# Keeping the gate's normalised rows and logits in SBUF for the experts' stage

## The reference

```python
logits = jnp.einsum('bsd,ed->bse', x, gate_w) + gate_b
probs = jax.nn.softmax(logits, axis=-2)            # over the 2048 tokens
vals, idx = top_k(probs, 8)                        # 8 tokens for each batch row and expert
tok = take_along_axis(x, idx)                      # rows of x
merged = jnp.einsum('bked,bke->bed', tok, vals)    # one row for each batch row and expert
h = gelu([merged, 1] @ w1[e])                      # w1: 32 x 257 x 1024
o = [h, 1] @ w2[e]                                 # w2: 32 x 1025 x 256
out = zeros.at[idx].add(o * vals)                  # back to the 8 tokens
```

## Time and profile before

| | |
|---|---|
| median of three runs | 5150.57 us |
| profiled execution: its span | 5142.3 us |
| median of the runs less this span (what lies around it) | 8.3 us |
| PE / DVE / ACT / POOL busy, share of the span | 92% / 82% / 67% / 26% |
| bytes moved by DMA | 498.42 MB |
| gate's stage | 575 to 755 us |
| experts' stage | 755 to 974 us |

### The profile page before, as it was taken

The page is one execution under the profiler, slowest core; times in us unless marked ns, Lnnn a source line. Parts: engine busy times, 40 slices in busy tenths (PEclk is TensorE's granted clock), DMA queues, the critical chain, the costliest instruction groups (busy, mean ns, idle before and its releaser), DMA issues. The chain is left out here.

```text
span 5142.3 us, 90411 instructions
## 1 busy us (share of the span) xinstructions
PE 4714.6 (92%) x34043; PEld 2092.5 (41%) x34043; DVE 4237.0 (82%) x5517; ACT 3449.7 (67%) x6176; POOL 1333.4 (26%) x881
## 2 busy tenths in 40 slices
PE   6999786797999999999999999999998879999993
PEld 3444452364333333333333333333334445555542
DVE  6999650397899999999999999999993877777736
ACT  4787310132688888888888888888886326666663
POOL 2233220164000000000000000000001229999992
PEclk9999897898899999999999999999998669999996
DMA  5110479688333333343333344333322941222305
GB/s 182 52 53 33 155 247 385 251 280 232 45 53 48 48 48 48 54 54 51 48 48 48 50 54 53 50 48 48 49 34 76 313 128 42 71 70 67 78 10 167
DMA packets 390773, 498.42 MB, mean 97 GB/s; under 512 B 165440, under 2 KB 278880, under 8 KB 373312
## 3 DMA queue, kind: packets, MB, share of 16 engines
q1 hardware_dynamic: 372448, 465.90, 38.7%
q10 hardware_dynamic: 17888, 26.74, 1.5%
HBM read 325.15 MB, written 165.02 MB: 95 GB/s over the span
## 5 line engine op out<-in xcount | busy, mean ns | idle before, releaser
L792 DVE TENSOR_REDUCE at_NM<-at_MX 128x1 f32<-128x1024 f32 (+1 forms) x3008 | 3085.0, 1050 | 299.5 <-PE at_MX L614 270.9
L734 ACT ACTIVATE at_PB<-at_S 128x512 f32<-128x512 f32 x5056 | 2719.4, 597 | 585.9 <-PE at_S L643 466.0
L614 PE MATMUL at_MX<-at_KT,at_QT 48*128 48x512 f32 (+1 forms) x5056 | 1919.7, 455 | 60.2 <-DMA at_VS<-v 45.6
L643 PE MATMUL at_S<-at_QT,at_KT 50*128 50x512 f32 (+1 forms) x5056 | 1899.9, 441 | 6.0 <-ACT at_PB L734 5.8
L655 PE MATMUL at_AV<-at_PB,at_VS 128*32 128x256 f32 (+1 forms) x18304 | 1567.7, 414 | 16.7 <-ACT at_AVS L742 15.7
L643 PEld LDWEIGHTS at_S<-at_QT,at_KT 50*128 50x128 f32 (+1 forms) x5056 | 801.8, 187 | 876.6 <-ACT at_PB L734 772.0
L614 PEld LDWEIGHTS at_MX<-at_KT,at_QT 48*128 48x128 f32 (+1 forms) x5056 | 791.6, 190 | 311.0 <-DVE at_NM L792 217.7
L655 PEld LDWEIGHTS at_AV<-at_PB,at_VS 128*32 128x32 f32 x18304 | 364.6, 108 | 858.6 <-ACT at_PB L734 745.4
L548 POOL CAST at_NMR<-at_NMF 16x128 fp32r<-16x128 f32 x79 | 22.1, 280 | 1625.3 <-ACT at_NMF L747 1625.3
L575 POOL TENSOR_TENSOR at_SUM<-at_SUM,at_PB 128x2048 f32<-128x2048 f32 x90 | 415.4, 4615 | 10.9
L932 PE MATMUL wkv_PQ<-wkv_XT,wkv_WT 128*128 128x512 f32 x768 | 339.6, 600 | 42.5 <-DVE wkv_DL L1052 25.9
(11 more groups left out here) (209 smaller groups left out, 3531.4 us busy)
## 6 DMA issues: line engine op xcount, KB each, us to landing
moe_W<-in_w SPq DMA_DIRECT2D x64, 1024.0 KB, 11.9
at_QT<-qk SPq DMA_DIRECT2D x402, 128.0 KB, 5.2
at_KT<-qk SPq DMA_DIRECT2D x384, 128.0 KB, 6.6
qk<-r_HI SPq DMA_DIRECT2D x52, 512.0 KB, 5.0
qk<-r_LO SPq DMA_DIRECT2D x52, 512.0 KB, 5.3
at_VS<-v SPq DMA_DIRECT2D x96, 256.0 KB, 9.2
at_KT<-qk SPq DMA_DIRECT2D x96, 256.0 KB, 6.2
ycat<-wkv_Y SPq DMA_DIRECT2D x32, 512.0 KB, 2.6
```

The costliest lines, as they stand in the source:

```text
L614: ins = nc.tensor.matmul(MX[r][:, a, :], q_of(s)[h:h + NQ, b * P:(b + 1) * P], k_of(it, s, b * P // W)[h:h + NQ, (c + a) * W:(c + a + 1) * W],
L643: nc.tensor.matmul(SP_[item(it, s, "score", t)[1]][:, :], k_of(it, s, c)[h:h + NQ + 2, kb * P:(kb + 1) * P], q_of(s)[h:h + NQ + 2, c * W:( ...
L734: nc.scalar.activation(PB[:, t % NPB, :], SP_[r][:, :], ACT.Exp, scale=scale).then_inc(exp_done, 1)
L792: nc.vector.tensor_reduce(NM4[:, b, c:c + 1], MX[r][:, :, :].rearrange("p a n -> p (a n)"), AX_X, ALU.max, negate=True).then_inc(ring_got, 1)
```

## The change

`rows`, a [128, 16, 4, 256] tile (64 KB in each partition), and `lg`, [128, 2048], are allocated around both stages. The gate's stage writes into them; the experts' stage reads them there. The DRAM tensors `xn2` and `logits`, their stores and their loads are gone. The bias GB now stands on all 128 partitions (four small loads), and PG has 128 rows, of which batch row b uses 32. After the merge the rows' space holds the second W2 buffer, HS, HT and OS, so `load(g)` is split, W2(1) waits for `merged`, and the clearing of HT waits for it too. The store of `routed` stands ahead of W2(1).

```diff
 # phase_gate
-        XN = [m.sb(f"XN{u}", [P, J, D]) for u in range(2)]
-        LG = [m.sb(f"LG{u}", [EXPERTS, GT]) for u in range(2)]
-        GB = m.sb("GB", [EXPERTS, 1])
-        PG = m.ps("PG", [EXPERTS, GT])
+        GB = m.sb("GB", [B * EXPERTS, 1])
+        PG = m.ps("PG", [B * EXPERTS, GT])
...
-            for dst, ap in ((ident[:, :], ident_d), (GW[:, :, :], ...), (GB[:, :], gb_d)):
+            for dst, ap in ((ident[:, :], ident_d), (GW[:, :, :], ...)):
                 sp.dma_start(dst, ap).then_inc(const_ld, 16)
+            for b in range(B):
+                sp.dma_start(GB[b * EXPERTS:(b + 1) * EXPERTS, :], gb_d).then_inc(const_ld, 16)
...
                 store(g)
-                if g > 0:
-                    store_normed(g - 1)
-                if g > 1:
-                    store_logits(g - 2)
-            store_normed(NGR - 1)
-            store_logits(NGR - 2)
-            store_logits(NGR - 1)
             for u in range(NX):
                 sp.wait_ge(x_st[u], 16 * len(range(u, NGR, NX)))
-            for u in range(2):
-                sp.wait_ge(n_st[u], 8 * NGR)
-                sp.wait_ge(l_st[u], 8 * NGR)
...
-                    ins = nc.tensor.matmul(PG[:, :], GW[:, c, :], XT[g % 2][:, c, :],
+                    ins = nc.tensor.matmul(PG[experts_of(g), :], GW[:, c, :], XT[g % 2][:, c, :],
...
+                es = experts_of(g)      # slice(g // E4 * EXPERTS, (g // E4 + 1) * EXPERTS)
                 wait(act, gated, g + 1)
-                wait(act, l_st[g % 2], 16 * (g // 2))
-                nc.scalar.activation(LG[g % 2][:, :], PG[:, :], ACT.Identity, bias=GB[:, 0:1]).then_inc(logits, 1)
+                nc.scalar.activation(lg[es, g % E4 * GT:(g % E4 + 1) * GT], PG[es, :], ACT.Identity,
+                                     bias=GB[es, 0:1]).then_inc(logits, 1)
...
                 wait(dve, rs1, g + 1)
-                wait(dve, turned, g - 1)
-                wait(dve, n_st[g % 2], 16 * (g // 2))
-                    ins = nc.vector.tensor_scalar(XN[g % 2][:, j, :], X[g % NX][:, j, :], ...
+                    ins = nc.vector.tensor_scalar(rows[:, g, j, :], X[g % NX][:, j, :], ...
 # phase_experts
-        XB = [m.sb(f"XB{u}", [P, B, 2, D]) for u in range(NX)]
-        W2 = [m.sb(f"W2{u}", [P, 4, HC, D]) for u in range(2)]
+        W2 = [m.sb("W20", [P, 4, HC, D]),
+              held_rows[:, 0:W2_END].rearrange("p (k c n) -> p k c n", k=4, c=HC)]
+        HS = held_rows[:, W2_END:HS_END]        # HT, OS behind it
...
-            def load(g):
-                u = g % 2
+            def load_w1(g):
                 wait(sp, h_put, g - 1)
...
+            def load_w2(g):
+                if g == 1:
+                    sp.wait_ge(merged, 1)
                 wait(sp, o_put, g - 1)
...
-            sp.dma_start(LG[:, :], lg_d.rearrange("b e t -> (b e) t")).then_inc(lg_ld, 16)
...
-            for g in range(2):
-                load(g)
+            load_w1(0)
+            load_w2(0)
+            load_w1(1)
             sp.wait_ge(w_done, 1)
             sp.dma_start(w_d.rearrange("b e t -> (b e) t"), LG[:, :]).then_inc(w_st, 16)
+            load_w2(1)
             for g in range(2, EG):
-                load(g)
+                load_w1(g)
+                load_w2(g)
...
+            pool.wait_ge(merged, 1)
             nc.gpsimd.memset(HT[:, :, :, :], 0.0).then_inc(zeroed, 1)
...
-            dve.wait_ge(lg_ld, 16)
             nc.vector.tensor_reduce(nmax[:, :], LG[:, :], AX_X, ALU.max, negate=True).then_inc(nmax_done, 1)
...
-            dve.wait_ge(zeroed, 6)
+            dve.wait_ge(zeroed, 5)      # the sixth ahead of the first copy to HT
...
-            for i in range(NX): load_x(i)            # and the other pairs after the exponential
...
-            for i in range(PAIRS):
-                wait(pe, x_ld[i % NX], 16 * B * (i // NX + 1))
-                ... XB[i % NX][:, b, k, :] ...
-                ins.then_inc(xb_used, 1)
+            for t in range(NB):
+                for b in range(B):
+                    ins = nc.tensor.matmul(PM[b * NE:(b + 1) * NE, 0:D], WTS[:, t, b * NE:(b + 1) * NE],
+                                           rows[:, b * E4 + t // J, t % J, :], start=(t == 0), stop=(t == NB - 1))
+            ins.then_inc(merged, 1)
```

More of the change, by code:

```diff
@@ L1114, with phase_gate @@
 HEADS2, DH2 = 8, 32
-def phase_gate(nc, y_d, ow_d, x_d, xnew_d, xn_d, ident_d, gw_d, gb_d, lg_d):
+def phase_gate(nc, y_d, ow_d, x_d, xnew_d, rows, lg, ident_d, gw_d, gb_d):
     E4 = T // GT
@@ L1147, in phase_gate, with experts_of @@
         x_ld, x_st = ([m.sem(f"{n}{u}") for u in range(NX)] for n in ("x_ld", "x_st"))
-        a_ld, n_st, l_st = ([m.sem(f"{n}{u}") for u in range(2)] for n in ("a_ld", "n_st", "l_st"))
+        a_ld = [m.sem(f"a_ld{u}") for u in range(2)]
         block = ctx.enter_context(nc.Block())
+        def experts_of(g):
+            return slice(g // E4 * EXPERTS, (g // E4 + 1) * EXPERTS)
         @block.sync
@@ L1166, in store @@
                 sp.dma_start(group(held(xnew_d), g), X[g % NX][:, :, :]).then_inc(x_st[g % NX], 16)
[L1168 to L1175, removed]
             sp.dma_start(OW[:, :, :], ow_d.rearrange("(q p) n -> p q n", p=P)).then_inc(ow_ld, 16)
@@ L1243, in turn @@
                         ins = nc.tensor.transpose(PT[:, c, j * P:(j + 1) * P],
-                                                  XN[g % 2][:, j, c * P:(c + 1) * P], ident[:, :])
+                                                  rows[:, g, j, c * P:(c + 1) * P], ident[:, :])
                     if c < CC - 1:
@@ L1259, in _ @@
             source(1)
[L1260 removed]
+            pe.wait_ge(const_ld, 16 * (2 + B))
             for g in range(NGR):
@@ L1325, in normed @@
                 wait(dve, rs1, g + 1)
[L1326 to L1327 removed]
                 for j in range(J):
[L1329 removed]
+                    ins = nc.vector.tensor_scalar(rows[:, g, j, :], X[g % NX][:, j, :], MV1[:, j, 0:1],
                                                   RS1[:, j:j + 1], ALU.subtract, ALU.mult)
@@ L2012, in _, with phase_experts @@
                 rope(g, 3)
-def phase_experts(nc, lg_d, xn_d, w1_d, w2_d, pick_d, ident_d, w_d, o_d):
+def phase_experts(nc, rows, LG, w1_d, w2_d, pick_d, ident_d, w_d, o_d):
     HID = 1024
@@ L2048, in phase_experts @@
         PO = m.ps("PO", [P, 512])
[L2049 to L2052, removed]
+        const_ld, nmax_done, zeroed, exp_done, soft, w_done, w_st, wt_put, wt_got = (m.sem(n) for n in (
+            "const_ld", "nmax_done", "zeroed", "exp_done", "soft", "w_done", "w_st", "wt_put", "wt_got"))
+        merged, ms_done, ms_turned, mts_done, me_done, pk_done, h_put, h_got, t_put, t_got, o_put, o_got, o_st = (
+            m.sem(n) for n in ("merged", "ms_done", "ms_turned", "mts_done", "me_done", "pk_done", "h_put", "h_got",
                                "t_put", "t_got", "o_put", "o_got", "o_st"))
         w1_ld, w2_ld = ([m.sem(f"{n}{u}") for u in range(2)] for n in ("w1_ld", "w2_ld"))
-        x_ld = [m.sem(f"x_ld{u}") for u in range(NX)]
-        xb_v = xn_d.rearrange("(b q p h i) d -> q h p b i d", b=B, p=P, h=J // 2, i=2)
         w1_v = w1_d[:, 0:D, :].rearrange("(g k) (c p) n -> g p k c n", k=4, p=P)
@@ L2113, in _ @@
                 nc.vector.tensor_copy(WTS[:, n * HC:(n + 1) * HC, :], TP[:, :, :]).then_inc(wt_got, 1)
-            dve.wait_ge(xb_used, PAIRS)
+            dve.wait_ge(merged, 1)
             nc.vector.tensor_copy(MS[:, :], PM[:, 0:D]).then_inc(ms_done, 1)
@@ L2149, in _ @@
         def _(act):
[L2150 to L2156, removed]
             act.wait_ge(nmax_done, 1)
@@ L2401, in sandwich @@
     ycat = dram("ycat", [2 * CC, P, TOK])
-    x1, xn2, x2, x3 = (dram(n, [TOK, D]) for n in ("x1", "xn2", "x2", "x3"))
-    logits, routed = (dram(n, [B, EXPERTS, T]) for n in ("logits", "routed"))
+    x1, x2, x3 = (dram(n, [TOK, D]) for n in ("x1", "x2", "x3"))
+    routed = dram("routed", [B, EXPERTS, T])
     expert_out = dram("expert_out", [B, EXPERTS, D])
@@ L2415, in sandwich @@
         phase_wkv(nc, xnT, d["rkv_w"], d["decay"], d["first"], ident, ycat)
-        phase_gate(nc, ycat, d["out_w"], d["x"], x1, xn2, ident, d["gate_w"], d["gate_b"], logits)
-        phase_experts(nc, logits, xn2, d["w1"], d["w2"], d["pick"], ident, routed, expert_out)
+        with nc.sbuf_tensor("rows", [P, NG, J, D], F32) as rows, nc.sbuf_tensor("lg", [B * EXPERTS, T], F32) as lg:
+            phase_gate(nc, ycat, d["out_w"], d["x"], x1, rows, lg, ident, d["gate_w"], d["gate_b"])
+            phase_experts(nc, rows, lg, d["w1"], d["w2"], d["pick"], ident, routed, expert_out)
         phase_rope(nc, routed, expert_out, x1, x2, ident, d["wqkv1"], d["rope"], qk1, v1)
```

32 lines of the change are left out of this document (14 added, 18 removed).

## The result

Four runs of the changed kernel gave 5115.17, 5120.91, 5122.11 and 5123.89 us, median 5121.51, against 5150.94 for the kernel before (four runs): ratio 0.9943, 95% interval 0.9929 to 0.9957. Forecast were 5123.1 us and a range of 5119 to 5129.5. The profiled execution is the shortest of the four: span 5113.4 us, 1.8 us of its own time lie around it. The 8.3 us that the prediction put around the span were thus mostly the spread between executions, which reaches ±10 us in what follows (six runs of one kernel lie between 5106.49 and 5127.03 us); it does not enter the difference. Where single microseconds matter, stages of profiled executions are compared, not whole runs.

The account below looks back on a forecast made before the run. The prediction took the experts' stage to be bound by its transfers: 23.5 (bytes) + 5.5 (gaps) - 1.5 (start of the flow) = 27.5 us, from 5150.57 to 5123.1 us, range 5119 to 5129.5.

Parts of the forecast that it names:

- Bound: Experts' stage is bound by its transfers, at 402 GB/s; the gate's stage is not.
- Gate's edits at 0: Gate's stage: dropped stores, new tile, PG's 128 rows and three more loads of GB change nothing, 0 us.
- Seam, 1.4 us: End of the gate's stage: without the last logits' store the experts' stage starts 1.4 us earlier.
- Bytes, 23.5 us: Experts' stage: 9.44 MB fewer to move, at 401.5 GB/s, save 23.5 us.
- Start of the flow, 759.6: Start of experts' stage: weights flow from 759.6 instead of 758.1, losing 1.5 us with the seam's gain included.
- The new wait: W2(1)'s wait for `merged`: merge ends between 783.6 and 788.0, before the DMAs run empty; no gap, 0 us.
- Gaps, 5.5 us: Experts' stage: DMA standstills at 826 to 831 and 841 to 843 us both go, saving 5.5 us.
- Steady pace as before: Experts' stage from hidden(3) on: each group takes the same 20.9 us as before.
- The work after W1(7)'s landing: End of the experts' stage: this work stays the same.
- the rivals: Gaps stay, 5128.6 us (15 in 100); order paces, 5142.0 us (3 in 100); queue behind `merged`, slower (2 in 100).
- the third: Rival: SP's queue stands behind `merged`; from a merge's end at 791.8 each microsecond costs one; 2 in 100.
- another stage changes its length: Sign that the prediction is wrong: a stage other than those it named changes its length.

Follow-up runs that it names:

- bytes experiment: Changed kernel plus six loads of 1 MB that nobody reads, ahead of load_w1(2) to load_w1(7): 5133.61 us, ratio 0.9978 to the kernel before.
- the kernel with the padding: Changed kernel with two unused 128-byte tiles per partition, shifting `rows` by 128 bytes and all behind `lg` by 256: 5114.20 us, ratio 0.9938 to the kernel before.
- the two kernels with less ahead of the wait: Changed kernel with W1(1) loaded after W2(1): 5130.88 us; changed kernel with 256-byte-aligned tiles and W1(0), W2(0) loaded in gate's stage: 5109.29 us, then 5115.70 us.

## Why the prediction was right

The forecast was 27.5 us; the stages gave 26.7 (218.9 - 194.1 = 24.9 in the experts' stage, 2.74 - 0.87 = 1.9 at the seam), the medians 29.4, within their interval of 22 to 37. Step by step:

- *Bound.* Right. The waits' view and the bytes experiment show it.
- *Gate's edits at 0.* Right as far as the runs tell: the loop is unchanged, and stores put back showed no cost that could be laid to them. The new kernel's first normalisation came 25.2 us after its stage's start, before 24.5; not the three loads of GB but the clock did that: the kernel with the logits through DRAM has the same loads and took 24.5, and TensorE's first 64 matmul records took 16.3 us in the new kernel, 15.7 before and 15.5 there.
- *Seam, 1.4 us.* It was 1.9; the barrier alone is 0.9, not the 1.3 inferred.
- *Bytes, 23.5 us.* The price per byte held (six loads of 1 MB, 6.29 MB, expected at 15.7 us, hidden(7) 15.5 later).
- *Start of the flow, 759.6.* SP's constants took 1.8 us instead of the assumed 3.0, W was issued at 756.4 and flowed from about 758.3 (0.92 MB moved by 760, 0.25 of them constants): 1.3 us better.
- *The new wait.* Merge's end 783.83 at the early end of 783.6 to 788.0. It held SP, not the DMAs. The lead of SP's issues, on which the margins rested, was inferred wrongly and to the safe side: `routed` was expected to be issued at 785.6, 6 us ahead of the end of the weights' transfers, and was issued at 776.75. The slow loads of W2(1) begin near 792, 8 us after their issue. Moving W1(1) behind the wait shows what a lack of cover costs.
- *Gaps, 5.5 us.* Both gone: between 760 and 930 no stretch of 2 us is below 348 GB/s.
- *Steady pace as before.* Wrong by size: 85.1 us from hidden(3) to hidden(7), not 83.6 (394 GB/s; the prediction called itself wrong under 390). "HS, HT and OS lie elsewhere but have the same shapes" was thought of; that W2's second tile lies elsewhere too was not costed at all. W2(1), W2(3) and W2(5) at about 350 instead of 387 GB/s are 3.0 us at hidden(7), which moving `rows` by 128 bytes gave back.
- *The work after W1(7)'s landing.* Taken as unchanged, it is 0.9 us longer (hidden(7) to the next stage: 27.06 us, 26.13 before), 0.65 of it hidden(7) at the lower clock for longer.

So hidden(3) came at 836.5 (forecast 837.4), being early by the flow, and hidden(7) at 921.6 (921.0), having lost that to the misaligned tile. Two small errors, of opposite sign, made the sum look better than its terms: that is luck, and the mechanism (bytes at the stage's rate, the gaps closed, the wait covered) is not. None of the rivals held. The point from which the third decides, a merge that ends too late for the queue ahead of the wait, was not reached in the changed kernel; it was in the two kernels with less ahead of the wait, and there its price rule, a microsecond for each microsecond that the DMAs stand still, holds (with W2(1) first, 10.6 us later for 10.2 lost).

What stays open: the span fell by 28.9 us, the stages named here by 26.7 less 0.8, by which the last logits came later. The rest, 3.0 us, lies behind them. The first attention alone is 5.3 us shorter than before (2680.6 against 2685.9 us) and the other stages behind the experts are together about 2.4 longer. No edit touches them, and executions of one and the same kernel differ there by more: in the changed kernel's two profiles the first attention took 2680.6 and 2688.6 us, with experts' stages of 194.1 and 194.2. So of the prediction's sign "another stage changes its length" nothing can be laid to the change, and the 29.4 us of the medians agree with 27.5 only within their interval.

## What to carry to other kernels

When a stage runs its DMAs at full share, price an edit by its bytes at that stage's own measured rate, and the same bytes at nothing in a neighbour with spare share; then moving loads into that neighbour is the next step. A tile laid over another's space inherits its start address: with pieces of 1 KB check in the built program that this is a multiple of 256 bytes. Behind a new wait in a queue, work out how long the DMAs are fed by what stands ahead of it, and also what the items behind it release.

## What the runs showed of the hardware

The rate of loads into SBUF at full DMA share depended on piece and start address: 4 KB pieces went at about 420 GB/s on a multiple of 256 bytes and at 410 at 128 past one, 1 KB pieces at 384 to 392 and at 347 to 353. Multiples of 256 that are not multiples of 512 did as well as those that are: W2's own tile is the one in the changed kernel (byte 178,944, 389 GB/s) and the other in the kernel with the padding (179,200, 387).

The granted clock (0.50 is the lower level, 1.2 GHz; 1.00 the upper, 2.4 GHz) made one and the same group of work take 7.0 us in one execution and 10.1 in another, after TensorE had waited 8 us for weights in both.
